# Local attention in one chip kernel: the scores moved to the end of TensorE's step, v's third matmul behind the turned outputs, VectorE's maxima last in its step

## What is computed

```python
for i in range(DEPTH):                       # DEPTH = 6
    x = attn_layer(shift_tokens(x), Wqkv[i], q_scale[i], k_scale[i], Wo[i]) + x
    x = ffn_layer(shift_tokens(x), ...) + x

def attn_layer(x, Wqkv, qs, ksc, Wo):
    q, k, v = jnp.split(x @ Wqkv, 3, -1)     # 16 heads of 64
    q, k = l2norm(q) * qs, l2norm(k) * ksc   # then rotary tables on q and k
    out = local_attention(q, k, v)           # windows of 32 queries, 64 keys: softmax(q k^T * 8) v
    return out @ Wo
```

## Time and profile before

| | |
|---|---|
| median of three runs | 5188.2 us (5182.22 to 5189.37) |
| profiled execution | 5190.46 us |
| its span | 5188.7 us |
| mean granted TensorE clock | 0.974 |
| busy | PE 4809.2 us (93%), DVE 3830.0 (74%), ACT 3400.6 (66%), POOL 2676.4 (52%) |

### The profile page before, as it was taken

One profiled execution on the slowest core, in us unless ns is written; L12 is line 12 of the kernel. 1 busy time (PEld: TensorE's weight loads), 2 busy tenths in 40 slices (PEclk: granted clock), 3 DMA queues, 4 the chain that ended last, 5 costly groups with the idle time before them and its releaser, 6 DMA issues. The chain is left out here.

```text
span 5188.7 us, 210326 instructions
## 1 busy us (share of the span) xinstructions
PE 4809.2 (93%) x84978; PEld 3960.3 (76%) x84978; DVE 3830.0 (74%) x7791; ACT 3400.6 (66%) x6983; POOL 2676.4 (52%) x3403
## 2 busy tenths in 40 slices
PE   6999999989999999999999999999999998788879
PEld 4888888877888788878887788878887886455557
DVE  4777777868888788878887788878887886455543
ACT  2333333337778777777777777777787776566664
POOL 1221222227667666766667666766676664222212
PEclk8999999999999999999999999999999999899889
DMA  1000000013222322232223222332222222000000
GB/s 45 8 8 8 8 8 8 8 38 85 69 68 68 90 69 68 69 87 70 68 68 87 70 68 68 74 84 68 68 74 73 67 69 53 1 0 0 0 0 17
DMA packets 422085, 254.09 MB, mean 49 GB/s; under 512 B 201104, under 2 KB 418734, under 8 KB 420799
## 3 DMA queue, kind: packets, MB, share of 16 engines
q1 hardware_dynamic: 415008, 234.97, 18.8%
q10 hardware_dynamic: 6688, 13.45, 0.8%
HBM read 25.08 MB, written 4.25 MB: 6 GB/s over the span
## 5 line engine op out<-in xcount | busy, mean ns | idle before, releaser
L1313 POOL TENSOR_TENSOR b_rot<-b_t 128x1024 f32<-128x1024 f32 x384 | 907.8, 2364 | 251.8 <-DVE b_t L1861 251.5
L1859 DVE TENSOR_TENSOR b_t<-psum,b_cosg 128x1024 f32<-128x1024 f32 x384 | 469.3, 1222 | 437.0 <-ACT b_sq L1701 429.4
L1329 POOL TENSOR_TENSOR b_qk<-b_rot,b_rnorm 128x1024 f32<-128x1024 f32 x384 | 730.8, 1903 | 41.7 <-issue 0.2
L1447 PE MATMUL psum<-b_w_hi,b_xT_parts 128*128 128x512 f32 x1152 | 524.4, 455 | 27.5 <-issue 18.2
L1701 ACT ACTIVATE b_sq<-psum 128x1024 f32<-128x1024 f32 x384 | 391.4, 1019 | 121.9 <-PE psum L1452 119.6
L1866 DVE TENSOR_REDUCE b_ss_floor<-b_sq 128x16 f32<-128x1024 f32 x384 | 463.9, 1208 | 0.0
L1452 PE MATMUL psum<-b_w_hi,b_xT_parts 128*128 128x512 f32 x1152 | 456.8, 397 | 0.0
L1448 PE MATMUL psum<-b_w_lo,b_xT_parts 128*128 128x512 f32 x1152 | 453.4, 394 | 0.2 <-issue 0.2
L1534 PE MATMUL psum<-shared,b_oT 128*128 128x128 f32 x3072 | 425.2, 281 | 0.8 <-ACT b_oT L1719 0.8
L774 ACT ACTIVATE a_probs<-psum,a_nbias 128x256 f32<-128x256 f32 x512 | 195.4, 487 | 347.5 <-DVE a_nbias L864 347.5
L1436 PE MATMUL psum<-ident,b_qk 128*128 128x128 f32 x3072 | 403.7, 274 | 13.9 <-DVE b_o L1898 13.8
(11 more groups left out here) (276 smaller groups left out, 12360.7 us busy)
## 6 DMA issues: line engine op xcount, KB each, us to landing
b_v_win<-b_v SPq DMA_DIRECT2D x2304, 65.0 KB
b_v_win<-b_v SPq DMA_DIRECT2D x1152, 32.5 KB
oa<-XR SPq DMA_DIRECT2D x1024, 2.0 KB
xcur<-X SPq DMA_DIRECT2D x111, 128.0 KB, 4.3
shared<-in_L_ffn_Wqkv_dram ACTq DMA_DIRECT2D x6, 1536.0 KB
b_x_shifted<-X SPq DMA_DIRECT2D x96, 64.0 KB
b_x_shifted<-X SPq DMA_DIRECT2D x96, 63.5 KB
shared<-in_L_ffn_Wo_dram SPq DMA_DIRECT2D x10, 256.0 KB, 3.4
```

The source lines that it names most:

```text
L1313: nc.gpsimd.tensor_tensor(rot[:, i, :, :], t1[:, i, :, :], t2[:, i, :, :], ALU.add).then_inc(rot_done, 1)
L1329: nc.gpsimd.tensor_tensor(qk[:, i, :, :], rot[:, i, :, :], rnorm[:, i, :, None].broadcast_to((P, 16, BD)), ALU.mult).then_inc(qk_done, 1)
L1447: nc.tensor.matmul(r, xT_hi[:, ts], w_hi[:, piece(hg, i)], start=True, stop=False)
L1859: nc.vector.tensor_tensor(t14, x4, tab(cosg, slice(0, BD), BD), ALU.mult)
```

## The change

TensorE: of `project_v` the two matmuls of the high part stay where they were, the third (the low part) goes behind `turn_outputs`. `scores` goes from behind `turn_probs` to behind `outputs`. ScalarE: `values` goes behind `turned_outputs` (and, in j = 2, behind the two gelus). VectorE: `residual` goes ahead of `normalise`, both ahead of `floor_squares`, and the maxima and their subtraction are last (in j = 0, 2 and 3 pieces of the feed-forward still follow). No instruction is added or removed; GpSimd's and SyncE's lists are as before.

```diff
@@ TensorE
-                    def project_v(s, m, new_layer):
+                    def project_v_by_high(s, m, new_layer):
...
                         by_high(bank_c, s, 2, new_layer)
+
+                    def project_v_by_low(s):
                         by_low(bank_c, s, 2).then_inc(v_full, 1)
...
                             if ok(j + 4):
-                                project_v(j + 4, m + 4, new_layer)
+                                project_v_by_high(j + 4, m + 4, new_layer)
...
                             if ok(j):
                                 turn_outputs(m, ok(j + 2))
+                            if ok(j + 4):
+                                project_v_by_low(j + 4)
                             if ok(j + 1):
                                 turn_probs(j + 1, m + 1, ok(j + 2))
-                            if ok(j + 2):
-                                scores(j + 2, m + 2, ok(j) and ok(j + 1))
...
                             if ok(j + 1):
                                 outputs(j + 1)
+                            if ok(j + 2):
+                                scores(j + 2, m + 2, ok(j) and ok(j + 1))
@@ ScalarE
-                            if ok(j + 4):
-                                values(part, n, j + 4, m + 4)
...
                             if ok(j):
                                 turned_outputs(m)
+                            if ok(j + 4):
+                                values(part, n, j + 4, m + 4)
@@ VectorE
                                 rotate(part, j + 4, m + 4, front)
+                            if j == 0 and output:
+                                ffn_residual(n - 2, before(b, 2))
+                            if ok(j):
+                                residual(b, j, m)
+                            if ok(j + 1):
+                                normalise(m + 1)
+                            if ok(j + 4):
+                                floor_squares(j + 4, m + 4)
                             if ok(j + 2):
                                 maxima(m + 2)
                                 less_maxima(j + 2, m + 2)
-                            if ok(j + 4):
-                                floor_squares(j + 4, m + 4)
-                            if j == 0 and output:
-                                ffn_residual(n - 2, before(b, 2))
-                            if ok(j + 1):
-                                normalise(m + 1)
-                            if ok(j):
-                                residual(b, j, m)
```

## The result

| | before | after |
|---|---|---|
| median | 5187.6 us | 6011.8 us (6004.43 to 6012.56, 4 runs) |
| span of the profiled execution | 5188.7 us | 6002.6 us |
| mean granted clock | 0.974 | 0.943 |

The ratio is 1.1588, with a 95% interval of 1.1568 to 1.1608: 824 us slower. The forecast was 5840 in a range of 5700 to 6040.

What follows compares the result with a forecast made beforehand. TensorE bounds the local layers, busy 480.5 of 500 us. A new ring of 40.0 us a sequence for 33.45 adds 622 us over 95 sequences to 5190.5, giving 5812; 30 for the clock makes 5840, range 5700 to 6040.

Steps and rivals of the forecast that it cites:

- The ring of waits: Scores, maxima, exponentials, squares, copy of q, turned outputs, Wo, outputs: longest chain of waits between steps, 40.0 us a sequence.
- Exponentials gate the squares: On ScalarE the next exponentials come 1.95 us behind the start of TensorE's step, and the squares stand behind them.
- The ring's lengths: Steps j = 0 to 3 take 9.4, 9.4, 11.2 and 10.0 us, together 40.0 a sequence for 33.45.
- VectorE's place in it: Floor and normalised outputs on VectorE, 1.19 us together, end at A + 5.0, ahead of the maxima.
- A + 5.08: A is the start of the turned outputs on TensorE; the maxima's start was forecast at A + 5.0.
- Wo's wait for v's copy: TensorE's product with Wo waits 0.5 us for ScalarE's copy of v, seen at A + 1.84.
- v's third matmul fills nothing: On TensorE, the moved matmul only makes the gap ahead of the turned outputs grow.
- The profile's signs: TensorE busy 80 to 83%, wait for q 400 to 560 us, rotation period 10.0 us; clock below 0.9 would refute.
- the forecast's own range: Ring as laid out with few falls of the clock: 5730 to 5920 us, chance 0.58.
- the second rival: TensorE's clock falls at most of the long gaps: 5920 to 6170 us, chance 0.2.
- the clock: TensorE's clock falls at some gaps of about 2 us in j = 1 and 2: 30 us in all.
- one gap in seven: Assumed share of the two long TensorE gaps a sequence where the clock falls, at 1.1 us each: 30 us.

Runs made afterwards that it cites:

- e5_exps_behind_q_and_k: The changed kernel with ScalarE's exponentials and mask behind the squares and the copies of q and k in j = 0, 1 and 3: 5647.2 us, ratio 1.0882.
- e2_scores_alone: The changed kernel with v's part undone on TensorE and ScalarE, scores and maxima still moved: 5960.8 us, ratio 1.1481.
- e9_scores_apart: The changed kernel with two extra matmuls of 512 columns between the products with values and the scores: 5975.9 us, ratio 1.1517.
- e3_filled_gaps: The changed kernel with six redundant matmuls of 512 columns ahead of v's in j = 1 and 2: 5909.8 us, ratio 1.1385.

## Why the prediction was right, and where its size was off

The ring of waits was right at each step. *Exponentials gate the squares*: the wait stands in 383 steps, and moving them and nothing else but the mask takes the steps j = 0, 1 and 3 from 9.56, 9.38, 10.00 (with the clock up) to 8.44, 8.55, 8.69. *The ring's lengths*: 9.4, 9.4, 11.2 and 10.0 were forecast; 9.57, 9.38, 11.26 and 10.00 were measured with the gaps filled and the clock mostly up, 40.2 for 40.0, and the changed kernel has the same lengths but for j = 1. *VectorE's place in it*: the maxima started at A + 5.08, after the normalised outputs as forecast; in the old order they wait for the scores. *Wo's wait for v's copy*: 0.49 for 0.5. *v's third matmul fills nothing*: + 0.45% alone in all steps. That was put too generally: v's part in j = 0 and 2 alone gains 0.35%.

The profile's signs: TensorE's busy share 81% (80 to 83 forecast), its wait for q 508 us (400 to 560), period 10.48 (10.0), clock 0.95 (above 0.9). The last of these was too blunt a sign: 122 falls leave the mean at 0.95.

The measured time is 172 us over the forecast, and 92 over the top of the forecast's own range, 5730 to 5920. The wide range, 5700 to 6040, holds it only because the larger part of the second rival had been added. The term that was mis-sized is the clock: I took one gap in seven, 27 falls and 30 us. There were 122, at 1.06 us each 129 us: 99 of the 172. The price of a fall, 1.1, came out, though it had been no more than a choice between 0 and 1.9. How often it falls I guessed too low, from one row of 1.92 us that held and one of 2.30 that fell. In j = 1, with a gap of 2.05 us in the median, it fell 80 times in 95; in j = 2, with 1.92, 21 times; and 20 times in j = 3, where the gap is 1.10 us and I had counted none. The second rival ("falls at most of the long gaps", 5920 to 6170, chance 0.2) holds the measured time; forecast and rival differ in nothing else. The page "TensorE: Matmul & The Clock Gate" of the Trainium skill, section "HAM oscillation — how this bites in real kernels", describes a kernel in which the wait between batches takes the clock down every time. The trace agrees with it in part: 101 falls at the 190 gaps of j = 1 and 2.

The rest is some 70 us. 20 come from the ring's 0.2 us. Some 30 more come from comparing a mean with a typical step. The 33.45 of before is a mean over all sequences, with long steps in it, while 40.0 was worked out from steps without them (medians before: 8.05 + 7.19 + 9.62 + 8.28 = 33.14). That is 0.31 x 95 = 30 us. The last 20 or so stay open. The stops within the scores, 52.4 us, are part of the long steps after; how much of them lengthens the ring is not shown. Open as well: why the clock fell at one gap of a given length and held at another.

## What to carry to other kernels

On an engine that works in order, an instruction that waits for late data sets the start of everything listed behind it: before a producer is moved to the end of a step, look at where its consumer stands on the other engine, and move that as well. To price such a move, follow one ring of waits from a step to the next step's same instruction, from rows; here it came out within 0.2 us of 40. Then ask what the gaps do to TensorE's clock, and compare means with means.

## What the runs showed of the hardware

The clock fell at some of TensorE's gaps and not at others of the same length. By step, with the gap ahead of the turned outputs in the median and the falls in some 95 steps:

| run, step | gap, us | falls |
|---|---|---|
| changed kernel, j = 1 | 2.05 | 80 |
| changed kernel, j = 2 | 1.92 | 21 |
| changed kernel, j = 3 | 1.10 | 20 |
| `e5_exps_behind_q_and_k`, j = 2 | 1.92 | 58 |
| `e2_scores_alone`, j = 1 | 1.81 | 53 |
| `e9_scores_apart`, j = 2 | 1.62 | 5 |
| `e9_scores_apart`, j = 1 | 1.59 | 5 |
| `e3_filled_gaps`, j = 3 | 1.11 | 16 |
| `e3_filled_gaps`, j = 1 | 0.67 | 4 |

A fall cost 1.06 us by the run with filled gaps. There six redundant matmuls in the gap, 1.4 us of work, paid for themselves: 102 us less. With the clock up the last of the four transposes of the outputs ended 0.66 us after the first began; with the clock down, 1.11 us.

TensorE stood still up to 2.2 us within a row of short matmuls (64x32 weights, 64 columns) without a wait, in 40 places when two such rows stood together and in 37 when 0.45 us of other work parted them. Before the change it stood still at such a row in 9 places, 1.3 us at most. The stops of more than 0.5 us in the changed kernel each end 1.0 to 1.5 us after a transfer of the instruction queue has ended; that they are waits for instructions is not shown.
